# Attention with 16 heads of 16: scores as 16-row products at every 32nd partition, without spreading the keys

## The reference, cut to what matters

```python
def _L1_xattn_ref(query, key, value, ...):          # 16 x 64 queries, 256 wide, 16 heads of 16
    q = apply_rope(proj(query, Wq, bq)); k = apply_rope(proj(key, Wk, bk)); v = proj(value, Wv, bv)
    q = q * Dh ** (-0.5)
    scores = jnp.einsum('bhqd,bhkd->bhqk', q, k)
    mask = (rel > 0) | (rel < -WINDOW)               # rel = key index - query index
    scores = jnp.where(mask, neg, scores)            # only keys 0 .. 63 are seen by 64 queries
    probs = jax.nn.softmax(scores, axis=-1)
    out = jnp.einsum('bhqk,bhkd->bhqd', probs, v)
    return out.transpose(0, 2, 1, 3).reshape(Bq, Sq, D) @ Wo.T + bo
```

## Time and profile before

| | us |
|---|---|
| median of 3 runs (lowest, highest) | 773.25 (772.59, 773.65) |
| the profiled execution, its own time | 772.14 |
| its span in the profile | 770.4 |
| PE busy in the span | 676.5 |
| DVE busy | 492.2 |
| ACT busy | 374.3 |
| POOL busy | 242.8 |

### The profile page before, as it was taken

How to read it: one execution, slowest core, us unless ns; L and a number is a source line. 1 busy time by engine, 2 the same in 40 slices (tenths; PEclk the granted TensorE clock), 3 DMA queues, 4 the chain that set the end, 5 groups by cost and what they waited for, 6 DMA issues and landing times. The chain is left out here.

```text
span 770.4 us, 10238 instructions
## 1 busy us (share of the span) xinstructions
PE 676.5 (88%) x3718; PEld 457.3 (59%) x3718; DVE 492.2 (64%) x775; ACT 374.3 (49%) x719; POOL 242.8 (32%) x167
## 2 busy tenths in 40 slices
PE   2999999989929988989888999986986959899998
PEld 2445555543326555655556888854554545699897
DVE  3223343458569989889894357899874665555455
ACT  2221111235498988889883333334672442544342
POOL 1000000000059998979770000456830130220000
PEclk9999999999969999999999999998997979799999
DMA  9989999818202332222200000000001120100000
GB/s 349 347 340 414 422 422 377 309 62 213 85 27 86 106 107 86 93 83 99 83 29 1 0 15 15 0 16 16 1 1 55 56 54 1 46 10 1 27 1 29
DMA packets 31046, 86.39 MB, mean 112 GB/s; under 512 B 7882, under 2 KB 19556, under 8 KB 28820
## 3 DMA queue, kind: packets, MB, share of 16 engines
q1 hardware_dynamic: 29892, 84.75, 30.4%
q10 hardware_dynamic: 1104, 0.98, 0.4%
HBM read 83.50 MB, written 1.11 MB: 110 GB/s over the span
## 5 line engine op out<-in xcount | busy, mean ns | idle before, releaser
L677 POOL TENSOR_TENSOR dbu<-du,bs 128x1024 f32<-128x1024 f32 x64 | 150.6, 2369 | 233.3 <-DVE du L867 215.4
L968 PE MATMUL Y<-weighed,ident 128*128 128x512 f32 (+1 forms) x256 | 101.3, 517 | 0.0
L877 DVE TENSOR_TENSOR_SCAN w_in<-A,dbu 128x1024 f32<-128x1024 f32 x42 | 95.2, 2276 | 0.1
L770 ACT ACTIVATE weighed<-T,CT 128x256 f32<-128x256 f32 x208 | 83.0, 472 | 22.5 <-PE T L958 20.0
L759 ACT ACTIVATE A<-delta,negA 128x504 f32<-128x504 f32 x128 | 83.0, 692 | 1.7 <-DVE xn L877 1.7
L968 PEld LDWEIGHTS Y<-weighed,ident 128*128 128x128 f32 x256 | 43.9, 192 | 29.8 <-issue 29.2
L958 PE MATMUL T<-ident,w_in 128*128 128x128 f32 x336 | 45.3, 279 | 12.3 <-ACT weighed L770 7.3
L958 PEld LDWEIGHTS T<-ident,w_in 128*128 128x128 f32 x336 | 37.4, 142 | 28.3 <-DVE w_in L877 14.8
L877 DVE TENSOR_TENSOR_SCAN xn<-A,dbu 128x1024 f32<-128x1024 f32 x22 | 50.1, 2278 | 1.0 <-issue 1.0
L312 PE MATMUL O<-cN,pT 128*64 128x256 f32 x384 | 46.7, 385 | 0.0
L300 PE MATMUL S<-cT,qkT 128*64 128x512 f32 (+1 forms) x256 | 45.6, 509 | 0.0
(11 more groups left out here) (340 smaller groups left out, 1385.3 us busy)
## 6 DMA issues: line engine op xcount, KB each, us to landing
cT<-in_ctxT SPq DMA_DIRECT2D x8, 3202.0 KB, 13.7
cN<-in_ctx SPq DMA_DIRECT2D x8, 3072.0 KB, 12.7
bs<-b_rows SPq DMA_DIRECT2D x32, 512.0 KB, 3.7
raw_w<-in_w SPq DMA_DIRECT2D x16, 256.0 KB, 3.1
w<-in_w SPq DMA_DIRECT2D x7, 256.0 KB, 8.2
vs<-vx SPq DMA_DIRECT2D x8, 136.0 KB, 2.4
x<-in_x SPq DMA_DIRECT2D x1, 1024.0 KB, 6.0
cR<-in_ctx SPq DMA_DIRECT2D x1, 1024.0 KB, 21.4
```

What stands on the lines that cost most here:

```text
L677: e.tensor_tensor(dbu[s % NB][:, :, :], half(m.du, s // DS), row, ALU.mult).then_inc(s_bu, 1)
L770: i = e.activation(weighed[s % 2][:, q * Q:(q + 1) * Q], T[:, q * Q:(q + 1) * Q], ACT.Copy, scale=c_of(s, q))
L877: e.tensor_tensor_scan(S[s % NS], A[s % 2][:, :], dbu[s % NB][:, :, :].rearrange("p c n -> p (c n)"), 0.0, ALU.mult, ALU.add).then_inc(s_h, 1)
L968: e.matmul(Y[:, w], k.ident[:, :], weighed[s % 2][:, w], start=False, stop=True, skip_group_check=True).then_inc(s_y, 1)
```

## The change

q and k of each head get a place of 32 columns in the rotated tile (`rot`, now a tile of its own), 16 of numbers and 16 of zeros that GpSimd clears once. VectorE writes it in two operations, q and k, so that after the transposes head h = 4j + c lies on partitions 32j to 32j + 15 of chunk c. Four chunks each for q and k make eight transposes, in two batches that use the same bank one after the other. The scores are one product for each head and batch, 16 rows by 64 columns by 64, in two parts: part 0 takes heads of j = 0 and 2, part 1 those of j = 1 and 3. Part 0 of a tile moves into the step before, behind `weigh`, and stands between the two batches of transposes. ScalarE copies q and k as 512 columns each. `spread_keys` is gone.

```diff
-        rot = [by_head(k.w_out[:, 2 * i:2 * i + 2, :].rearrange("p c d -> p (c d)")) for i in range(2)]
-        kb = [sb(f"hkb{i}", [P, 2, KD, HG * L]) for i in range(2)]
+        rot = [sb(f"hrot{i}", [P, 2 * H, SPAN]) for i in range(2)]
...
-            def turn_rotated(t):
-                e.wait_ge(s_rt, t + 1)
-                if t >= 1:
-                    e.wait_ge(s_qe, t)
+            def turn_rotated(t, part):
+
+                if part == 0:
+                    e.wait_ge(s_rt, t + 1)
+                    if t >= 1:
+                        e.wait_ge(s_ke, t)
...
                 else:
-                    ac("x2", 3)
-                if t - 4 >= 0:
-                    e.wait_ge(s_oe, t - 3)
-                for c in range(2 * KD):
-                    j = e.transpose(T[1][:, c * P:(c + 1) * P], rot[t % 2][:, c * HG:(c + 1) * HG, :].rearrange("p h d -> p (h d)"),
-                                    k.ident[:, :])
+                    e.wait_ge(s_qe, t + 1)
+                for c in range(HC):
+                    at = part * H + c * P // SPAN
+                    j = e.transpose(T[1][:, c * P:(c + 1) * P],
+                                    rot[t % 2][:, at:at + P // SPAN, :].rearrange("p h d -> p (h d)"), k.ident[:, :])
                 j.then_inc(s_tq, 1)
 
-            def scores(t):
-                e.wait_ge(s_kb, t + 1)
-                if t == 0:
-                    ac("y", 3)
-                if t >= 2:
-                    e.wait_ge(s_sm, t - 1)
-                for g in range(KD):
-                    for b in range(2):
-                        e.matmul(S[t % 2][64 * b:64 * b + 64, g * HALF:(g + 1) * HALF], qT[t % 4][:, g, 64 * b:64 * b + 64],
-                                 kb[t % 2][:, b, g, :], start=True, stop=False, skip_group_check=True)
+            def scores(t, part):
...
+                if part == 0:
+                    e.wait_ge(s_ke, t + 1)
+                    if t == 0:
+                        ac("y", 3)
+                    if t >= 2:
+                        e.wait_ge(s_sm, t - 1)
+                else:
+                    e.wait_ge(s_sa, t + 1)
+                for c in range(HC):
+                    for j in (part, part + 2):
+                        rows, h = slice(j * SPAN, j * SPAN + DH), j * HC + c
+                        for b in range(2):
+                            i = e.matmul(S[t % 2][64 * b:64 * b + 64, h * L:(h + 1) * L], qT[t % 4][rows, c, 64 * b:64 * b + 64],
+                                         kT[t % 4][rows, c, 64 * b:64 * b + 64], start=part == 0 and c == 0, stop=False,
+                                         skip_group_check=True)
...
             def step(i):
                 if tile(i):
-                    scores(i)
+                    scores(i, 1)
...
                 if tile(i + 2):
-                    turn_rotated(i + 2)
+                    turn_rotated(i + 2, 0)
                 if tile(i - 1):
                     weigh(i - 1)
+                if tile(i + 1):
+                    scores(i + 1, 0)
+                if tile(i + 2):
+                    turn_rotated(i + 2, 1)
...
+            turn_rotated(0, 0)
             project(1)
-            turn_rotated(0)
+            turn_rotated(0, 1)
...
-            turn_rotated(1)
+            turn_rotated(1, 0)
+            scores(0, 0)
             keys_and_values(2)
+            turn_rotated(1, 1)
...
-            def move_rotated(t):
-                e.wait_ge(s_tq, t + 1)
-                src = T[1][:, :].rearrange("p (c n) -> p c n", n=P)
+            def move_rotated(t, part):
+                e.wait_ge(s_tq, 2 * t + part + 1)
                 if t >= 4:
                     e.wait_ge(s_sc, t - 3)
-                e.activation(qT[t % 4][:, :, :], src[:, 0:KD, :], ACT.Copy)
-                if t >= 2:
-                    e.wait_ge(s_kb, t - 1)
-                e.activation(kT[t % 2][:, :, :], src[:, KD:2 * KD, :], ACT.Copy).then_inc(s_qe, 1)
+                dst = (qT, kT)[part][t % 4]
+                e.activation(dst[:, :, :], T[1][:, :].rearrange("p (c n) -> p c n", n=P), ACT.Copy
+                             ).then_inc((s_qe, s_ke)[part], 1)
...
+            for r in range(2):
+                e.memset(rot[r][:, :, DH:SPAN], 0.0).then_inc(s_z, 1)
...
-                e.tensor_tensor(rot[t % 2][:, :, :], t1[t % 2][:, :, :], t2[t % 2][:, :, :], ALU.add).then_inc(s_rt, 1)
+                by_row = lambda a: a.rearrange("p (q j c) d -> p q j c d", q=2, j=P // SPAN)
+                for q in range(2):
+                    i = e.tensor_tensor(rot[t % 2][:, :, 0:DH].rearrange("p (q c j) d -> p q j c d", q=2, c=HC)[:, q],
+                                        by_row(t1[t % 2])[:, q], by_row(t2[t % 2])[:, q], ALU.add)
+                i.then_inc(s_rt, 1)
```

More of the change, by code:

```diff
@@ L1061 @@
 OPS = 14
+SPAN = 32
+HC = H * SPAN // P
 LEAD = 3
@@ L1096, in ffn_and_heads @@
         t1, t2 = ([by_head(k.w_in[:, j, i * HALF:(i + 1) * HALF]) for i in range(2)] for j in range(2))
-        rot = [by_head(k.w_out[:, 2 * i:2 * i + 2, :].rearrange("p c d -> p (c d)")) for i in range(2)]
-        qT = [sb(f"q4T{i}", [P, KD, P]) for i in range(4)]
-        kT = [sb(f"k4T{i}", [P, KD, P]) for i in range(2)]
-        kb = [sb(f"hkb{i}", [P, 2, KD, HG * L]) for i in range(2)]
+        rot = [sb(f"hrot{i}", [P, 2 * H, SPAN]) for i in range(2)]
+        qT = [sb(f"q4T{i}", [P, HC, P]) for i in range(4)]
+        kT = [sb(f"k4T{i}", [P, HC, P]) for i in range(4)]
         mx = [sb(f"hmx{i}", [P, H]) for i in range(2)]
@@ L1125, in ffn_and_heads @@
         s_qe = sem("h_qe")
-        s_kb = sem("h_kb")
+        s_ke = sem("h_ke")
+        s_sa = sem("h_sa")
         s_sc = sem("h_sc")
@@ L1299, in scores @@
[L1299 to L1308 removed]
+            def turn_rotated(t, part):
[4 more added lines that the diff above has]
+                    else:
+                        ac("x2", 3)
+                    if t - 4 >= 0:
+                        e.wait_ge(s_oe, t - 3)
+                else:
+                    e.wait_ge(s_qe, t + 1)
[3 more added lines that the diff above has]
+                                    rot[t % 2][:, at:at + P // SPAN, :].rearrange("p h d -> p (h d)"), k.ident[:, :])
+                j.then_inc(s_tq, 1)
@@ new lines, in scores @@
+            def scores(t, part):
[5 more added lines that the diff above has]
+                        e.wait_ge(s_sm, t - 1)
+                else:
+                    e.wait_ge(s_sa, t + 1)
[6 more added lines that the diff above has]
+                                         skip_group_check=True)
+                if part == 0:
+                    i.then_inc(s_sa, 1)
+                    return
@@ L1342, in turn_out @@
                 e.wait_ge(s_on, t + 1)
-                e.wait_ge(s_qe, min(t + 4, TILES))
+                e.wait_ge(s_ke, min(t + 4, TILES))
                 if t >= 1:
@@ L1466, in move_values @@
                 if p == 0:
-                    e.wait_ge(s_z, 3)
+                    e.wait_ge(s_z, 5)
                 pe("vp", p)
@@ L1538, in step @@
                 if tile(i + 2):
-                    move_rotated(i + 2)
+                    move_rotated(i + 2, 0)
+                    move_rotated(i + 2, 1)
                 if tile(i):
@@ L1569, in _ @@
             move_y(2)
-            move_rotated(0)
+            move_rotated(0, 0)
+            move_rotated(0, 1)
             squares(3)
@@ L1574, in _ @@
             move_y(3)
-            move_rotated(1)
+            move_rotated(1, 0)
             move_values(2)
+            move_rotated(1, 1)
             move_normed3(2)
@@ L1606, in sines @@
                 e.tensor_tensor(t2[t % 2][:, :, hd:DH], k.qkb[:, t, :, 0:hd], sn[1], ALU.mult).then_inc(s_sn, 1)
-            def spread_keys(t):
-                e.wait_ge(s_qe, t + 1)
-                if t >= 2:
-                    e.wait_ge(s_sc, t - 1)
-                for c in range(KD):
-                    for b in range(2):
-                        j = e.tensor_tensor(kb[t % 2][:, b, c, :].rearrange("p (h n) -> p h n", n=L),
-                                            kT[t % 2][:, c, b * L:(b + 1) * L].unsqueeze(1).to_broadcast([P, HG, L]),
-                                            k.own_head[:, :].unsqueeze(2).to_broadcast([P, HG, L]), ALU.mult)
-                j.then_inc(s_kb, 1)
-            sines(0)
-            spread_keys(0)
-            sines(1)
-            sines(2)
-            for i in range(TILES):
-                if tile(i + 1):
-                    spread_keys(i + 1)
-                if tile(i + LEAD):
-                    sines(i + LEAD)
+            for t in range(TILES):
+                sines(t)
         @block.vector
@@ L1745, in rotate @@
                 if t >= 2:
[L1746 to L1747 removed]
+                    e.wait_ge(s_tq, 2 * (t - 1))
+                by_row = lambda a: a.rearrange("p (q j c) d -> p q j c d", q=2, j=P // SPAN)
[3 more added lines that the diff above has]
+                i.then_inc(s_rt, 1)
```

1 line of the change is left out of this document (removed).

## The result

The changed kernel takes 787.63 us (median of 4 runs, 779.23 to 789.47) beside 772.92 for the kernel before; the ratio is 1.0181, interval 1.0098 to 1.0264. In another session it was 785.08 (9 runs) beside 772.71, ratio 1.0134 [1.0093, 1.0174]. It is slower, by both intervals, and both medians lie above the range of the forecast (769.5 to 782), though single runs went down to 778.06.

The account below looks back on a forecast made before the run. VectorE was taken to bound the front of the heads' stage, TensorE the loop behind. A 4.3 us lead, then 1.04 lost each loop step, ended the stage 2.2 us later: 775.4 us from the median, range 769.5 to 782.

Parts of the forecast that it names:

- Part 1: Front of the heads' stage: without GpSimd's key spread VectorE runs faster, so rotate(3) comes 4.3 us earlier; 2.6 us wait stays.
- Part 2: Score products in the loop: 1.05 us a part of 32 records, 2.10 a tile against 1.87, so +0.23 us.
- the first rival: Score products: all four array places overlap, 0.44 us a part, 5.8 us less in all, 769.7 us; chance 0.27.
- Part 3: Loop's transposes and ScalarE copies: k's copy delays the exponential, turn(i, 0) waits 0.24; a step takes 8.28 us against 7.24.
- I assume that 2.6 us of waiting don't bring it down: TensorE's remaining wait for rotate(3), steps 1 and 2: the granted clock was assumed not to fall; costed at nothing.
- The rival: Clock falls in the 2.6 us wait for rotate(3): 2.6 us more ahead of tile 1's exponential, 778.0 us; chance 0.12.
- falls in the loop: Loop of tiles: short products replace dense ones and the clock falls; two steps at half clock give 787 us; chance 0.05.
- my sum: Whole heads' stage, step by step: it ends 2.2 us later, giving 774.3 from the profiled run, 775.4 from the median.
- The lead: TensorE's time gained at rotate(3), 4.3 us, used up by slower loop steps: weigh(4) at 560.7 instead of 560.48.

Follow-up runs that it names:

- the four profiles: The changed kernel, unaltered, profiled four times: stage 115.10, 110.80, 112.66 and 115.11 us, against 106.29 us in the kernel before.

## Why the prediction was wrong

**Part 1 was right.** The third rotated tile's transposes were due at 525.05; they began at 529.02, which on the time base of before is 524.4 (4.6 off, the difference of the first marks), a lead of 4.9 us for 4.3. The wait left over was 3.13 for 2.6. The run without most of the spread shows 3.2 of the lead with the rest of the kernel untouched.

**Part 2 was mis-sized.** 32 records take 0.62 us, not the 1.05 that I took from the nearest rows: two row groups side by side, 0.90 without. This was the mechanism of the first rival, at a price between its 0.44 and mine. That is 19 ns a record. The Trainium skill (TensorEngine Tiling (Array Packing), Theoretical Speedup) points the right way: it gives up to 4 times for 32 rows, and the second row group gave 0.90 / 0.62 = 1.45 here. The 25 ns that the Trainium skill gives as the least between two starts (TensorE: Matmul & The Clock Gate, Part 1) doesn't hold for these records.

**Part 3 was right in its mechanism.** A step was to take 8.28 us with a wait of 0.24. With 0.62 for 1.05, TensorE is 0.86 earlier at `turn` (two parts) and the exponential 0.43 (one part lies ahead of it): 0.24 + 0.43 = 0.67 of wait, 8.28 - 0.43 = 7.85 a step. Measured: 0.70 and 7.93. Half of what faster products save returns as a wait.

**The step that failed is "I assume that 2.6 us of waiting don't bring it down", said of the clock.** My evidence was 1.53 us of idleness at full clock; between 1.53 and 7.06 no row stood, and I gave the fall 0.12. In the sum it stands at nothing, and so does every later fall. Filling the wait kept the clock at 1.00, which shows that the wait brings it down. The rival put the price of the fall at 2.6 us, and `weigh(1)` came 2.7 late, but the size agrees by luck: from a start 0.6 early, 1.8 us were lost up to `turn(1, 0)`, where the rival had all of its 2.6, and another 1.6 between `turn(1, 0)` and `weigh(1)`, where it had none. What I did not see is that the clock stays low for 10.2 to 13.7 us, and that the waits which part 3 itself predicts (2.13 behind a table load, then 1.22 ahead of `weigh(5)`) bring it down again; I had given falls in the loop 0.05:

| mark | forecast | measured less 4.6 |
|---|---|---|
| `weigh(1)` | 534.4 | 537.1 |
| `turn(2, 0)` | 541.7 | 544.35 |
| `weigh(2)` | 544.5 | 548.5 |
| `weigh(4)` | 560.7 | 564.0 |
| `turn(5, 1)` | 568.3 | 571.2 |
| next stage | 594.0 | 600.6 |

The gap opens by 2.7 at the first fall, 1.3 at the second, closes by 1.1 over the shorter steps, and opens by 3.7 over the third and the stage's end. With the measured price of a part and the clock at 1.00 my sum would have been 2.2 - 5.8 x 0.43 / 0.61 = -1.9 us, a slight gain; the stages measured are 6.4 to 10.7 above that. The clock can account for this by an estimate: from the mean clock of the stages it stands at 0.50 for some 13 us before (0.94) and some 24 to 35 in the four profiles (0.89 to 0.85). Half of the excess, if TensorE bounds all of it, is some 6 to 11 us. No run has the early copy of k and a clock of 1.00 throughout, so the -1.9 itself is not shown.

The lead was to be spent at `weigh(4)`, 0.2 us late; there it was 3.5 late (564.0 beside 560.48). The copy of k costs 0.92 us a step at full clock, which part 3 had in its mechanism; the rest of the 6.7 to 11 us that its move gave lies, as argued and not measured apart, in the falls of the clock behind its waits.

## What to carry to other kernels

Where a change replaces dense products by narrow ones or transposes, price each wait of TensorE behind it twice: once as the wait, once as the low clock that may follow, which here lasted 3 to 14 us. Before merging two producers into one PSUM bank, look at who waits in order behind the second copy; moving that copy behind the work which TensorE needs next gave 6.7 to 11 us of the stage here, more than the change had cost (4.5 to 8.8). A spread or a copy taken off a side engine pays only if the operations it slowed are on the path, so test it alone first: here it gave 3.8 us of the stage by itself.

## What the runs showed of the hardware that was not expected

- The granted clock fell to 0.50 behind waits of 3.13 and of 1.22 us in every profile of the changed kernel (ahead of the 1.22 stood short products and waits of 0.70), and behind the same wait of 2.13 us in two of four. It fell behind a wait of 1.57 us in the kernel with the wait filled, and not behind one of 1.53 in the kernel before: the length of the wait alone does not tell.
- Counted from the end of the wait for the third rotated tile, it came back after some 3 us under 128x512 products (one run), after some 5 under the old scores, and after 10.4 to 13.4 mostly under transposes and products of 34 to 64 columns, where TensorE counts as busy 5.98 of the first 6.00 us.
- Records of 64 columns on two alternating row groups start 19 ns apart (0.62 us for 32); on one group 28 ns (0.90).
- Unchanged stages behind this one took 175.7 to 182.6 us in different runs, with a mean granted clock of 0.93 at the short end and 0.89 to 0.90 at the long one.
